# A four-layer attention and feed-forward kernel on one core: layer-2 attention spaced wider, the first gate loaded first, and layer-3 query and value copies on ScalarE

## The reference

```python
# layer 1, gated block: groups of 256 tokens in the original shape, causal softmax attention
rw = gating(x, sim_matrix, gates)                       # [tokens, 16 experts], softmax over active experts
q = einsum('btc,ech,bte->bth', x, q_proj, rw)           # k and v likewise
out = einsum('bth,ehc,bte->btc', attention(q, k, v), o_proj, rw)

# layer 2 attention: each token first picks its best context token
qp = x @ Wq.T; idx = argmax(qp @ kv.T); mem = kv[idx]
mk, mv = split(mem @ Wkv.T); logits = heads(qp) @ mk.T * scale
out = (softmax(logits) @ mv) @ Wc.T

# layer 3 attention: a query sees keys seg-4 .. seg of its sequence's 64
keep = (key <= seg) & (key >= seg - LOOKBACK)           # LOOKBACK = 4
attn = softmax(where(keep, q @ k.T * scale, -inf)); out = (attn @ v) @ Wo
```

## Time and profile before

| | us |
|---|---|
| median of 3 runs | 3215.64 (3213.81 to 3218.95) |
| profiled execution | 3212.88 |
| its span, first to last instruction | 3211.1 |
| PE busy | 2643.7 (82% of the span) |
| PEld busy | 1759.5 (55%) |
| DVE busy | 2083.1 (65%) |
| ACT busy | 1277.0 (40%) |
| POOL busy | 518.9 (16%) |

### The profile page before, as it was taken

The page is one execution under the profiler, slowest core; times in us unless marked ns, Lnnn a source line. Parts: engine busy times, 40 slices in busy tenths (PEclk is TensorE's granted clock), DMA queues, the critical chain, the costliest instruction groups (busy, mean ns, idle before and its releaser), DMA issues. The chain is left out here.

```text
span 3211.1 us, 66655 instructions
## 1 busy us (share of the span) xinstructions
PE 2643.7 (82%) x24651; PEld 1759.5 (55%) x24686; DVE 2083.1 (65%) x5077; ACT 1277.0 (40%) x1968; POOL 518.9 (16%) x941
## 2 busy tenths in 40 slices
PE   4867679995999999999997888877979776777357
PEld 3634346663566566566664555555657554555227
DVE  6789769993454554554544677776840386877784
ACT  3558768870000000000001656553543343443264
POOL 0012210000000000000000000001421434666204
PEclk9988789997999999999998888887999898999789
DMA  3110000002311311211210000000013220000001
GB/s 91 30 61 1 0 25 15 13 7 106 106 53 55 105 53 60 98 53 64 94 53 12 15 11 10 10 1 29 27 34 105 79 62 3 0 0 0 8 0 52
DMA packets 55129, 128.60 MB, mean 40 GB/s; under 512 B 9669, under 2 KB 21317, under 8 KB 53962
## 3 DMA queue, kind: packets, MB, share of 16 engines
q1 hardware_dynamic: 47466, 106.36, 10.0%
q0 software_dynamic: 7520, 20.34, 2.1%
HBM read 109.37 MB, written 17.30 MB: 39 GB/s over the span
## 5 line engine op out<-in xcount | busy, mean ns | idle before, releaser
L1418 PE MATMUL banks<-l1f_xe,l1f_w 128*128 128x512 f32 x1024 | 486.1, 597 | 10.7 <-DVE l1f_xe L1617 10.7
L1617 DVE TENSOR_TENSOR l1f_xe<-l1f_hT,l1f_rwb 128x512 f32<-128x512 f32 x256 | 173.5, 693 | 299.4 <-PE banks L1420 276.9
L1420 PEld LDWEIGHTS banks<-l1f_w,l1f_xe 128*128 128x128 f32 x2048 | 269.1, 192 | 123.0 <-issue 123.0
L1623 DVE TENSOR_TENSOR l1f_ae<-l1f_aoT,l1f_rwb 128x512 f32<-128x512 f32 x256 | 172.8, 691 | 160.2 <-PE banks L1448 155.7
L1420 PE MATMUL banks<-l1f_w,l1f_xe 128*128 128x128 f32 x2048 | 269.9, 275 | 0.0
L1418 PEld LDWEIGHTS banks<-l1f_xe,l1f_w 128*128 128x128 f32 x1024 | 177.0, 192 | 141.4 <-issue 126.8
L1448 PE MATMUL banks<-l1f_ae,l1f_w 128*128 128x512 f32 x512 | 225.0, 598 | 1.4 <-DVE l1f_ae L1623 1.4
L214 POOL COPY x<-xn 128x512 f32 (+1 forms) x16 | 9.8, 611 | 972.1 <-DVE xn L1647 972.1
L1448 PEld LDWEIGHTS banks<-l1f_ae,l1f_w 128*128 128x128 f32 x512 | 97.0, 192 | 118.1 <-issue 115.9
L1097 DVE TENSOR_REDUCE l2a_top<-banks 128x16 f32<-128x1024 f32 x64 | 78.3, 1224 | 64.8 <-PE banks L1044 64.3
L1044 PE MATMUL banks<-l2a_kbd,l2a_qT 64*64 64x512 f32 x512 | 82.2, 715 | 45.6 <-DVE l2a_prob L1100 45.6
(11 more groups left out here) (499 smaller groups left out, 6197.7 us busy)
## 6 DMA issues: line engine op xcount, KB each, us to landing
l1f_rwb<-l1f_shares SPq DMA_DIRECT2D x128, 512.0 KB, 4.5
l0a_ctxT<-in_ctxT SPq DMA_DIRECT2D x16, 256.0 KB, 2.6
l2f_sent<-l0f_zero SPq DMA_DIRECT2D x4, 1024.0 KB, 7.0
l1a_ctxT<-in_ctxT SPq DMA_DIRECT2D x16, 256.0 KB, 2.6
l2c_ctxT<-in_ctxT SPq DMA_DIRECT2D x16, 256.0 KB, 2.6
l2e_rows<-l2f_sent SPq DMA_DIRECT2D x16, 256.0 KB, 2.9
l2f_answers<-l2e_y POOLq DMA_DIRECT2D x16, 256.0 KB, 2.7
l3p_ctxT<-in_ctxT SPq DMA_DIRECT2D x16, 256.0 KB, 2.6
```

The costliest lines, as they stand in the source:

```text
L1418: pe.matmul(bank, w[:, n, e, :], xe[:, e % NB, :], start=(e == 0), stop=(e == E - 1))
L1420: last = pe.matmul(v_bank[:, D * j:D * j + D], xe[:, e % NB, P * j:P * j + P], w[:, 2, e, :], start=(e == 0 and j == 0), stop=(e == E - 1) ...
L1617: dve.tensor_tensor(xe[:, e % NB, :], hT[:, m, :], rwb[:, m, e, :], ALU.mult).then_inc(s.xe_ready, 1)
L1623: dve.tensor_tensor(ae[:, e % NB, :], aoT[:, m, :], rwb[:, m, e, :], ALU.mult).then_inc(s.ae_ready, 1)
```

## The change

There are three parts, in three phases.

**Layer-2 attention.** All core lags grow by two (12 to 15 become 14 to 17). `new_x` is split into `add_x` (lag 17) and `stats_x` (lag 18), and `spread_v` moves from lag 10 to 15. The POOL lags follow (16 to 18 and 9 to 10).

**Gated block.** The two small gate weights are loaded before the four 1 MB projections and have a semaphore of their own; PE waits for the projections only at the first `qkv`. The attention of a group moves one step earlier, from the `qkv` loop of the next step into the `out` loop of its own.

**Layer-3 attention.** ACT now copies queries (`copy_q`) and values (`copy_v`) and computes |key + 2 - seg| (`distance`); POOL compares it with 2 and multiplies the keys by the head mask, and that is all. The matmul that adds the mask now multiplies the 0/1 result by a diagonal of -1e30 (`never`) in place of the identity.

```diff
@@ attention_core (layer 3)
+            if mask:
+                mask.prepare(pool)
...
-                if mask and mask.copy:
-                    mask.copy(pool, t, par, s.score_psum)
+                if mask:
+                    mask.make(pool, t, par, s.score_psum)
...
-                pool.tensor_copy(qT[:, par], r.qT[:, bass.ds(P * t, P)]).then_inc(s.q_ready, 1)
-
-            def prepare_v(t, j):
...
-            pipeline(pool, k.NT, [(5, copy_mv), (2, add_bias), (0, prepare), (2, prepare_v)], unroll=TG)
+            pipeline(pool, k.NT, [(5, copy_mv), (2, add_bias), (0, prepare)], unroll=TG)
...
+                pe.wait_ge(s.qT_ready, t + 1)
...
-                        pe.matmul(scores[:, a], k.identb[:, :], rhs, start=True, stop=False, skip_group_check=True)
+                        pe.matmul(scores[:, a], never[:, :], rhs, start=True, stop=False, skip_group_check=True)
...
+            act.activation(never[:, :], k.ident, ACT.Copy, scale=NEG).then_inc(s.never_ready, 1)
+            act.wait_ge(s.cleared, 1)
+
+            def copy_q(t, j):
+                wait(act, s.score_psum, t - 1)
+                settle(act, k)
+                act.copy(qT[:, j % 2], r.qT[:, bass.ds(P * t, P)]).then_inc(s.qT_ready, 1)
+                if mask:
+                    mask.distance(act, t, j % 2)
+
+            def copy_v(t, j):
...
+            pipeline(act, k.NT, [(0, copy_q), (2, copy_v), (2, copy_pT), (1, exp)], unroll=TG)
...
@@ phase_l3_attention
+        def distance(act, t, par):
+            act.wait_ge(middle_ready, 1)
+            wait(act, ready, t - 1)
+            settle(act, k)
+            act.activation(off[:, par], middle[:, :], ACT.Abs, bias=r.segments[:, bass.ds(t, 1)], scale=-1.0).then_inc(measured, 1)
+
         def make(pool, t, par, used):
+            pool.wait_ge(measured, t + 1)
             wait(pool, used, t - 1)
...
+            pool.tensor_scalar(away[:, par], off[:, par], LOOKBACK / 2, None, ALU.is_gt).then_inc(ready, 1)
@@ phase_l1_ffn
+            sp.dma_start(sim[:, 0, :], k.dram["L1_ffn_sim_matrix"]).then_inc(s.gate_weights, 16)
+            sp.dma_start(gates[:, :], k.dram["L1_ffn_gates"]).then_inc(s.gate_weights, 16)
             for n, name in enumerate("qkvo"):
...
-            pe.wait_ge(s.weights, 16 * 6)
-
+            pe.wait_ge(s.gate_weights, 16 * 2)
...
+                    pe.wait_ge(s.weights, 16 * 4)
...
-                if live(2):
-                    for e in range(E):
+                for e in range(E):
+                    if e == 3 and live(1):
+                        score(n - 1)
+                    if e == 12 and live(1):
+                        turn_p(n - 1)
+                    if e == 15 and live(1):
+                        weigh(n - 1)
+                    if live(2):
                         out(n - 2, e)
...
-                    if e == 7 and live(2):
-                        centre(n - 2)
-                    if e == 9 and live(2):
-                        normalise(n - 2)
...
-                if live(2):
-                    for e in range(E):
+                for e in range(E):
+                    if e == 6 and live(1):
+                        centre(n - 1)
+                    if e == 9 and live(1):
+                        normalise(n - 1)
+                    if live(2):
                         weigh_ao(n - 2, m(2), e)
@@ phase_l2_attention
-            pipeline(dve, k.NT, [(12, lambda t, r: core.centre(dve, t, r)), (14, lambda t, r: core.normalise(dve, t, r)),
-                                 (15, lambda t, r: core.new_x(dve, t, r)), (6, at_group(choose)), (8, at_group(store_v)),
-                                 (10, at_group(spread_v))],
+            pipeline(dve, k.NT, [(14, lambda t, r: core.centre(dve, t, r)), (16, lambda t, r: core.normalise(dve, t, r)),
+                                 (17, lambda t, r: core.add_x(dve, t, r)), (6, at_group(choose)), (8, at_group(store_v)),
+                                 (18, lambda t, r: core.stats_x(dve, t, r)), (15, at_group(spread_v))],
```

More of the change, by code:

```diff
@@ L37 @@
 Residents = namedtuple("Residents", "qT kT v2 segments")
-Mask = namedtuple("Mask", "rhs copy", defaults=(None,))
+Mask = namedtuple("Mask", "rhs make distance prepare")
 OneHot = namedtuple("OneHot", "top index hot")
@@ L1726, in keep_q @@
                 pool.tensor_copy(core.qT[:, u, :], q[:, u, :]).then_inc(s.q_ready, TG)
[L1728 removed]
+            pipeline(pool, k.NT, [(18, lambda t, r: core.copy_mv(pool, t, r)), (10, at_group(keep_q))], unroll=RING, behind=8)
         @block.tensor
```

95 lines of the change are left out of this document (40 added, 55 removed).

## The result

The changed kernel takes 3116.8 us (median of 4 runs, 3114.3 to 3118.4) against 3216.3 (4 runs, 3213.8 to 3219.0): ratio 0.969, 95% interval 0.9673 to 0.9707. 3117 was predicted. The sum is right, but in part by luck: layer-3 attention was put 19 us too high, and layer-2 attention (8 us) and an unedited last phase (7 us) made up for most of it.

The account below looks back on a forecast made before the run. PE was taken to bound the gated block, DVE's pile-up layer-2 attention, POOL layer-3 attention. Terms -57 (layer 2), -38 (layer 3) and -3 (gated block) sum to -98: 3212.9 to 3115, median 3117 us, range 3095 to 3145.

Parts of the forecast that it names:

- Layer-2 attention, -57: Layer-2 attention: 4.4 us a round won (long step 2.6, clock staying up 1.8) over 13.5 rounds, +2 for longer pipeline.
- The spreading: hidden: Layer-2 attention: the moved spread copies (0.46 us) delay one `centre`, hidden by PE's query and value work.
- Round: 3 x 3.87 + 5.9 = 17.5: Layer-3 attention: three tiles of 3.87 us and a fourth of 5.9 with `new_x`, against 20.0 a round.
- the ring: Layer-3 attention: loop of PE score and DVE `centre`, next bound after POOL, score starts 3.87 us apart.
- rival A: Both attention phases: clock keeps falling behind idle pieces; layer 2 wins 33, layer 3 8; 3172 us; chance 0.09.
- (a): Gated block's start: gate weights loaded first are there when DVE is ready, near 736.3: -10.7 us.
- (b): Gated block's first attention: no output matmuls to hide under, PE waits out the chain: +8, and +1 for the clock.
- (c): Gated block's end: bare attention chain gone, last outputs start near 1718, not 1726.2, not at low clock: -10 us.
- (d): Gated block, 15 steps: attention among output matmuls costs PE about 0.6 us at the tenth matmul: +9 (0 to +20).
- B: Layer-2 attention: idle spread over all steps keeps TensorE at 1.2 GHz; slower, about 3335 us; chance 0.03.
- C: Gated block's output loop binds on DVE, all 3.1 us show instead of 0.6: 37 on top, 3154 us; chance 0.04.
- D: Layer-2 attention: re-spacing gives nothing, another stage (ACT at `keys`) is late; layer 3 alone wins: 3175 us; chance 0.04.

Follow-up runs that it names:

- e8: Kernel before, with 8 unread 128x128 matmuls added on PE once a round of layer-2 attention: 3190.2 us, ratio 0.9918.
- e11: Changed kernel, with two unread 128x512 POOL copies added beside `choose` in layer-2 attention: 3124.6 us.
- e10: Changed kernel, with layer-2 attention's two spread copies (`spread_v`) back in the step of `choose`: 3142.9 us.
- e6: Changed kernel, with 8 unread 128x128 matmuls added on PE in every fourth tile of layer-3 attention: 3117.1 us.
- e5: Changed kernel, with layer-3 attention's addition and statistics in two tiles instead of one: 3093.9 us.
- e4: Changed kernel, with the gated block's attention put back where it was, gate weights still loaded first: 3112.7 us.
- e9: Changed kernel, with layer-2 attention's addition and statistics together again, in the step where the addition now is: 3125.4 us.

## Why the prediction was right, and where it was not

**What bounds the kernel.** Held. PE bound the gated block, DVE's pile layer-2 attention, POOL layer-3 attention; each part alone moved its own phase, and the layer-2 part the last one besides.

**Layer-2 attention, -57.** Mechanism right, size 8 to 10 short. Round 21.5 to 22.5 forecast, 21.55 measured; score at 1.09. The clock's part was put at 1.8 a round, 24 us. e8 shows at least 27, and by its rounds with the clock up 2.35 a round (26.75 less 24.4), an estimate of 32 in 13.5 rounds. The pile's part was put at 2.6 a round; it is 2.85 (24.4 less 21.55). In the range 5 us were left for `choose`, shortened by 0.4 because POOL's copy left it. L1849 took 0.82 only in every other round of the kernel before and 0.59 in the rest, so it came to some 3 us. The Trainium skill (GPSIMD Engine Reference, section 1, Specifications) has the rule: GpSimd contends with DVE instructions that have two SBUF inputs. The same instruction at 0.42 in the profile after (L1862) and at 0.59 in e11 (L1872) bears it out. "The spreading: hidden" held only where it was put; e10 shows that the same 0.44 us would have cost 24.

**Layer-3 attention, -38.** This step failed. POOL left the path as said and the chain over ACT was short enough: the distance took 0.34 us and the copy 0.28 (0.3 assumed), and the chain ended 1.1 us early. What failed is "Round: 3 x 3.87 + 5.9 = 17.5", in two terms.

The first is the ring. In a round with the clock up the tiles take 4.15, 4.05, 3.91 and 6.06, 18.2 in sum, and 16 rounds of it are 11 us more. It is not mainly the pile that slows them: the ring runs at 4.06 before the first pile too. In three tiles of four PE starts 0.25 us after DVE's subtraction and not 0.10, and these 0.45 us are two thirds of the 0.7 a round. The prediction had put PE's new wait for `qT_ready` at nothing ("covered by the later `q_ready`"). Wherever the delay is 0.25, two semaphore instructions of PE start behind the end of the subtraction (as at 2633.69 and 2633.80); where it is shorter, and in the kernel before where POOL is not late, there is one at most. Whether the new wait brought them there no run shows, since none takes it away.

The second is the clock. The idle piece of 2.5 us that I saw coming ("some 2 in the fourth tile of layer 3") dropped it in 10 of 14 rounds: 10.8 us by e6. This is rival A's mechanism, in the phase for which it priced 2 of 2.5 us a round; it came at 0.7. I had treated the same pile as a cost in layer 2 and as harmless in layer 3. e5, which splits it, gives 17.4 and 43 us in all. That this is near the 17.5 of the term is luck: its tiles are not three of 3.87 and one of 5.9.

**Gated block, -3.** Right in sum (-5.0) and nearly so in each part: (a) start 10.0 earlier (10.7); (b) first projections of the second group at 814.43 (near 814), at low clock (3.33 us); (c) last outputs at 1723.77 (near 1723) and 14.00 us long, not 16.55; (d) 0.29 us a step at the tenth matmul, not 0.6, and PE's wait for `l1f_ae` 7.1 us in sum (near 9). By e4 the move costs 4 to 5 us, not the 8 of (b) to (d).

**What nobody had in the sum.** The last phase, -7.3. So 3117 came out of 8 us in layer 2 and 7 in the last phase that were not forecast, and 19 in layer 3 that did not come; the gated block gave 2 more than forecast. The range for layer 3 (-28 to -44) did not hold 18.7; the range of the whole did.

**The rivals.** B, C and D did not come. A came in layer 3 alone, at a third of its price there; in layer 2 the clock stayed up in all twelve full rounds of the profile after.

## What to carry to other kernels

Price a pile-up on the vector engine twice: by what it adds to its step, and by what PE's clock loses behind the wait (at least 27 of 65 us in layer 2, 10.8 in layer 3); and where one phase is worth splitting, look for the same instructions in its sister. Look where in a phase a gain lies, in the rounds or at its end: e9 had the size forecast and another place. Read a change by phases and not by the total: here an untouched loop moved 7 us and hid a gain of 11.
